# Layer 2's attention scores: half-size batches, each split, turned and copied several chunks ahead of its first use

## The reference, cut to what matters

```python
z = jnp.einsum('ni,hif->nhf', h, W)
el = jnp.einsum('nhf,hf->nh', z, a_l)
er = jnp.einsum('nhf,hf->nh', z, a_r)
e = jax.nn.leaky_relu(el[src] + er[dst], NEG_SLOPE)
m = jax.ops.segment_max(e, dst, num_segments=N)
ex = jnp.exp(e - m[dst])
s = jax.ops.segment_sum(ex, dst, num_segments=N)
alpha = ex / s[dst]
out = jax.ops.segment_sum(alpha[:, :, None] * z[src], dst, num_segments=N)
```

## Time and profile before

| what | us |
| --- | --- |
| median of 3 runs | 3153.91 (3153.67 to 3155.99) |
| the profiled execution | 3143.41 |
| its span, first to last instruction | 3141.5 |
| chunk 0's first reduce on DVE | starts at 1286.10 |
| chunk 351's last fold into `by_node` | starts at 1719.99, two instructions, 0.36 |
| first gather of the next stage on POOL | starts at 1722.49 |

### The profile page before, as it was taken

How to read it: one execution, slowest core, us unless ns; L and a number is a source line. 1 busy time by engine, 2 the same in 40 slices (tenths; PEclk the granted TensorE clock), 3 DMA queues, 4 the chain that set the end, 5 groups by cost and what they waited for, 6 DMA issues and landing times. The chain is left out here.

```text
span 3141.5 us, 50069 instructions
## 1 busy us (share of the span) xinstructions
PE 2774.9 (88%) x13690; PEld 2153.1 (69%) x13690; DVE 2489.0 (79%) x5349; ACT 1571.3 (50%) x3053; POOL 1639.9 (52%) x1473
## 2 busy tenths in 40 slices
PE   4999969999996997998988999999999595599997
PEld 3788734444445776776766788888888484488886
DVE  8656769999997676577777999999999785577775
ACT  3555623333334525333333677777777451266664
POOL 1788746666663572777773444444444230044443
PEclk9999989999998998999999999999999797699999
DMA  5433489999992032111111778778877551499997
GB/s 184 113 93 107 143 303 347 348 350 353 349 335 59 1 134 55 36 23 23 22 23 34 260 261 259 260 260 261 260 263 255 175 201 58 183 297 297 289 293 194
DMA packets 193609, 609.60 MB, mean 194 GB/s; under 512 B 41979, under 2 KB 51570, under 8 KB 189758
## 3 DMA queue, kind: packets, MB, share of 16 engines
q0 software_dynamic: 135040, 429.23, 43.3%
q1 hardware_dynamic: 58430, 178.63, 16.2%
HBM read 522.69 MB, written 84.86 MB: 193 GB/s over the span
## 5 line engine op out<-in xcount | busy, mean ns | idle before, releaser
L649 POOL DMA_INDIRECT g_rows<-z_rows,edge_src x704 | 696.6, 990 | 608.5 <-PE g_totals L1473 314.7
L1090 POOL DMA_INDIRECT shared<-el_rows,edge_src x352 | 336.7, 957 | 179.6 <-issue 107.0
L690 ACT ACTIVATE g_scaled_hi<-g_rows,edge_weight_sorted 128x1024 fp32r<-128x1024 f32 x176 | 202.7, 1151 | 355.3 <-DMA g_rows<-z_rows,edge_src 345.3
L704 PE MATMUL g_sums<-g_rows,g_share 128*128 128x512 f32 x704 | 332.2, 594 | 22.9 <-DMA g_rows<-z_rows,edge_src 22.9
L1466 PE MATMUL g_sums<-g_rows,g_share 128*128 128x256 f32 x1408 | 348.9, 391 | 0.0
L321 POOL DMA_INDIRECT edge_list<-payload,row_i x196 | 260.6, 1330 | 124.6 <-issue 115.9
L1418 ACT ACTIVATE g_scaled_hi<-g_rows,g_factor 128x256 fp32r<-128x256 f32 x704 | 299.9, 496 | 4.3 <-DMA g_rows<-z_rows,edge_src 2.1
L1542 DVE SCALAR_TENSOR_TENSOR g_scaled_lo<-g_rows,g_factor,g_scaled_hi 128x256 fp32r<-128x256 f32 x704 | 293.4, 479 | 1.7 <-ACT g_scaled_hi L1418 1.6
L1466 PEld LDWEIGHTS g_sums<-g_rows,g_share 128*128 128x128 f32 x1408 | 255.4, 191 | 27.8
L1321 DVE TENSOR_REDUCE t_largest<-t_masked 128x4 f32<-128x512 f32 x352 | 231.5, 685 | 51.9 <-PE t_masked L1172 44.6
L725 DVE SCALAR_TENSOR_TENSOR g_scaled_lo<-g_rows,edge_weight_sorted,g_scaled_hi 128x1024 fp32r<-128x1024 f32 x176 | 225.5, 1281 | 47.3 <-ACT g_scaled_hi L690 44.1
(11 more groups left out here) (396 smaller groups left out, 7494.1 us busy)
## 6 DMA issues: line engine op xcount, KB each, us to landing
e_raw<-in_L_ffn_rw_dram SPq DMA_DIRECT2D x56, 1024.0 KB, 6.8
g_rows<-z_rows,edge_src POOLq DMA_INDIRECT x704, 5.6
z_rows<-z_zout SPq DMA_DIRECT2D x20, 512.0 KB, 3.1
x_rows<-x_all SPq DMA_DIRECT2D x20, 512.0 KB, 2.6
z_rows<-t_zout SPq DMA_DIRECT2D x20, 512.0 KB, 2.7
s_x<-x_rows SPq DMA_DIRECT2D x20, 512.0 KB, 7.1
xn_rows<-s_rows SPq DMA_DIRECT2D x10, 1024.0 KB, 4.1
z_x<-in_x_dram SPq DMA_DIRECT2D x19, 512.0 KB, 4.1
```

The costliest lines, as they stand in the source:

```text
L649: pool.indirect_dma_start(out=r.rows[:, slot, :], out_offset=None, in_=table, in_offset=bass.IndirectOffsetOnAxis(ap=g.src[:, i * GT + q:i ...
L704: nc.tensor.matmul(sums[:, k, h, :], share[:, k, :], r.rows[:, k * GT, h * HALF:(h + 1) * HALF], start=True, stop=False)
L1090: q.indirect_dma_start(out=g.edge_el[:, n, :], out_offset=None, in_=g.el, in_offset=bass.IndirectOffsetOnAxis(ap=g.src[:, n:n + 1], axis=0 ...
```

## The change

Layer 2's batches become smaller and are prepared earlier:

- `BATCH` is 16; `BATCHES` lists the sizes: 21 batches of 16 and two of 8, so 23 in place of 11. `BATCH_AT` is the first chunk of each, `BATCH_OF` the batch of each chunk.
- A batch's three steps no longer stand at its first chunk `at`: the split on DVE stands ahead of take `at`-7, the turn on PE ahead of mask `at`-5, the copy on ACT ahead of chunk `at`-4's `set_apart`.
- `Z_FIRST` is 80 in place of 160, and the remaining 880 products are spread up to chunk 343 (`spread` = 344).

POOL's instructions are the same; only the semaphores that the landings count on differ.

```diff
-BATCH = 32
-NB = NE // BATCH
+BATCH = 16
+BATCHES = (BATCH,) * (NE // BATCH - 1) + (BATCH // 2, BATCH // 2)
+NB = len(BATCHES)
+BATCH_AT = tuple(sum(BATCHES[:b]) for b in range(NB))
+BATCH_OF = tuple(b for b in range(NB) for _ in range(BATCHES[b]))
+SPLIT_BEFORE = {max(0, at - 7): b for b, at in enumerate(BATCH_AT)}
+TURN_BEFORE = {max(0, at - 5): b for b, at in enumerate(BATCH_AT)}
+COPY_BEFORE = {max(0, at - 4): b for b, at in enumerate(BATCH_AT)}
...
-Z_FIRST = 160
+Z_FIRST = 80
...
-    spread = NE - BATCH // 2
+    spread = NE - BATCHES[-1]
...
-                ).then_inc(el_in[n // BATCH], 16)
+                ).then_inc(el_in[BATCH_OF[n]], 16)
...
-                b = n // BATCH
-                if n % BATCH == 0:
+                b = BATCH_OF[n]
+                if n == BATCH_AT[b]:
                     pe.wait_ge(rows_ready, b + 1)
...
-                    if n % BATCH == 0:
-                        turn_rows(n // BATCH)
+                    if n in TURN_BEFORE:
+                        turn_rows(TURN_BEFORE[n])
                     mask_chunk(n)
...
-                at_least(act, masked_ready, BATCH * (b - 1))
+                at_least(act, masked_ready, BATCH_AT[b - 1] if b else 0)
...
-                    if n % BATCH == 0:
-                        rows(n // BATCH)
+                    if n in COPY_BEFORE:
+                        rows(COPY_BEFORE[n])
...
-                dve.wait_ge(el_in[b], 16 * BATCH)
+                size = BATCHES[b]
+                dve.wait_ge(el_in[b], 16 * size)
...
-                    if n % BATCH == 0:
-                        parts(n // BATCH)
+                    if n in SPLIT_BEFORE:
+                        parts(SPLIT_BEFORE[n])
                     take(n)
```

More of the change, by code:

```diff
@@ L1171, in mask_chunk @@
                          start=True, stop=False)
-                t.matmul(masked[:, n % 3, :], pick[:, n % BATCH:n % BATCH + 1].to_broadcast([P, P]), el_rows[:, b % 2, :], start=False, stop=True).then_inc(masked_ready, 1)
+                t.matmul(masked[:, n % 3, :], pick[:, n - BATCH_AT[b]:n - BATCH_AT[b] + 1].to_broadcast([P, P]), el_rows[:, b % 2, :], start=False, stop=True).then_inc(masked_ready, 1)
             turn_tile(0, NT)
@@ L1310, in parts @@
             def parts(b):
-                dve.wait_ge(el_in[b], 16 * BATCH)
+                size = BATCHES[b]
+                dve.wait_ge(el_in[b], 16 * size)
                 at_least(dve, rows_turned, b - 1)
-                whole = g.edge_el[:, b * BATCH:(b + 1) * BATCH, :].rearrange("p n h -> p h n")
-                st.link(v.tensor_copy(el_parts[:, b % 2, :, 0, :], whole))
-                v.tensor_tensor(el_parts[:, b % 2, :, 1, :], whole, el_parts[:, b % 2, :, 0, :].bitcast(F32),
+                whole = g.edge_el[:, BATCH_AT[b]:BATCH_AT[b] + size, :].rearrange("p n h -> p h n")
+                st.link(v.tensor_copy(el_parts[:, b % 2, :, 0, 0:size], whole))
+                v.tensor_tensor(el_parts[:, b % 2, :, 1, 0:size], whole, el_parts[:, b % 2, :, 0, 0:size].bitcast(F32),
                                 ALU.subtract).then_inc(parts_ready, 1)
```

## The result

The changed kernel took 3136.14 us (median of 6 runs, 3128.98 to 3143.10) against 3153.79 for the kernel before (6 runs, 3145.50 to 3156.34). The ratio is 0.9948 with a 95% interval of 0.9928 to 0.9968: 17.7 us less, with an interval of about 10 to 23. The forecast was 13.4 less, 3140.5.

The account below looks back on a forecast made before the run. Gathers were taken to bind up to take 313: chunk 335 lands at 1660.9, then 45.4 us of work and 0.7 of lag end the stage at 1707.0 against 1720.35. That is 13.4 us less, 3140.5; range 3129 to 3148.

Parts of the forecast that it names:

- Which engine binds: In the chunk stage, gathers at 20.1 us per 16 chunks bind up to take 313; DVE and PE work sets the rest.
- The rate: DVE and PE work per batch of 16 chunks in the new order: 19.4 us, against 20.1 for the gathers.
- The coupling: DVE and PE coupled by three banks only: waits inside batches, 0.6 us per 16 chunks.
- PE's extra share: PE's share in a batch of 16 chunks grows by 3 matmuls, 0.7 us.
- the slack: Up to take 313, DVE's time spent waiting for gathers: 11 us over 20 boundaries, 0.7 us each.
- The last stretch: From chunk 335's landing: batch 20's split, then chunks 313 to 351, 45.4 us, with 0.7 of lag added.
- lag: Lateness left over from PE's half clock, added to the end of the stage: 0.7 us.
- The start: First reduce on DVE at 1269.7 in place of 1286.10, 16.4 us earlier, with 80 fewer products ahead of chunk 0.
- The first (gathers bind to the last): Rival: take 337 waits for the very last gather; stage ends at 1695.2, 25 us less, 3128.8; under 3136, chance 0.17.
- The second (gain given back at 20.5 per 16): Rival: engines run late throughout at 20.5 us per 16 chunks; 2 us less, 3152; within 6 us, chance 0.09.
- The third (half clock behind each boundary): Rival: each of 21 gather waits costs 3.1 us through the clock; 40 us more, 3194; over 6 us slower, chance 0.05.
- My argument against the rival: If DVE is late for the gathers, it does not wait; PE's stand shrinks to the split's 0.5 us, clock stays.

Follow-up runs that it names:

- the lead alone: Changed kernel with 11 batches of 32 and 160 leading products, spread up to chunk 335: stage 485.1 us, whole 3149.30, ratio 0.9982 to the kernel before.
- 160 leading products: Changed kernel with `Z_FIRST = 160` in place of 80: stage 466.5 us against 471.2, whole 3139.10 in one run.
- The removal of the waits: Changed kernel with splits reading a constant tile, DVE waiting for all gathers only behind the last chunk: stage 451.8 us against 471.2, whole 3116.20.
- kernel without a lead: Changed kernel with split, turn and copy at a batch's first chunk again: stage 537.2 us, whole 3202.31, ratio 1.0136 to the kernel before.
- the two kernels made for it: Changed kernel with 104 leading products, spread to chunk 319, or 160, spread to 311: 3561.98 and 3569.44 us on slow chips, 0.9902 and 0.9927 of the kernel before.

## Why the prediction was right

**Which engine binds.** Predicted: gathers to take 313, then work. Measured: 15 waits for landings, the last one ahead of take 313, none at takes 329 and 337 (1680.08 and 1689.62). In time: take 313's split at 1660.16 - 1233.12 = 427.0 us behind the first gather, predicted 1660.9 - 1235.8 = 425.1. It is 1.9 late. 1.1 of it is POOL's beat: the last gather was issued 443.9 behind the first in place of 442.8. The rest is the landing: chunk 335's gather started at 1656.87 and the split 3.3 us later, where I took the median of 2.4; with the lead alone and with 160 leading products the same distance was 3.2. The removal of the waits (451.8) and the late start that cost nothing (466.5) show the step, not only its numbers.

**The rate.** I took 19.4 us per 16 chunks. Measured 19.1 beside gathers, 18.8 without them, and 18.4 with 37 products per 16 chunks in place of 41 (the run's own expectation says 38). The coupling and PE's extra share, 0.6 and 0.7 of it, were a little too high. I had sized the slack accordingly too small, 11 us over 20 boundaries or 0.7 each; it was 24.6 in 15 waits, 1.6 each. This moves no term of the sum, since the landing of chunk 335's gather sets take 313 either way.

**The last stretch.** Predicted 45.4 and 0.7 of lag, measured 44.2. It began at half clock (0.88 over the 14 us from 1658 to 1672), so the lag was real, and the sum without it 1 to 2 us too long, as the rate is.

**The sum.** 425.1 + 46.1 = 471.2 predicted, 427.0 + 44.2 = 471.2 measured. That they agree to a tenth is luck: +1.9 and -1.9 cancel. The whole moved by 17.7 where 13.4 was carried over, within the interval of about 10 to 23; the stage can't tell what the 4 us are, and the rest of the program varies by more than that between executions.

**The start.** Predicted 16.4 earlier; 50.3 - 34.7 = 15.6 behind the first gather. It entered nowhere in the sum, and rightly: the run with 160 leading products shows it to be worth nothing here.

**Terms.** A split took 0.5 (0.22 and 0.26, overlapping slightly in the next), the turn 0.6 to 0.75. Both as taken.

**The rivals.** The first (gathers bind to the last) didn't come: behind take 313, 43.7 us of work remain even without gather waits. The second (gain given back at 20.5 per 16) needed the clock to cost as much per boundary as before; it cost less, 9 us at 1.2 GHz in place of 28. The third (half clock behind each boundary) did not happen in the changed kernel, 0.99. In the kernel without a lead, 0.94, the clock fell behind 16 of 20 boundaries, though at about 1.2 us of loss each (60 x 0.455 over 22) and not the 3.1 of the rival; that its 3202 us lie near the rival's 3194 is luck, since the stops came back too. The Trainium skill, "TensorE: Matmul & The Clock Gate", HAM oscillation, describes a loop in which each burst of matmuls waits for a transfer and starts again at half rate. The trace agrees in part: in the kernel without a lead most bursts do restart so, but what they wait for is DVE and ACT; in the changed kernel, with as many batches, transfers are waited for and the clock falls behind 2 of 22 boundaries. My argument against the rival, that where DVE is late PE's stand shrinks and the clock stays, is borne out by the kernel without gather waits (3.9 us of stands, clock 0.99). It needs the lead: without it PE stood 40.7 us for splits though no gather was waited for.

## What to carry to other kernels

Here a transfer stream ran a few per cent slower than the engines (20.1 against 19.1 us per 16 chunks). Taking out the stops between the engines then only moved the wait to the stream, until the batches shrank too. In both kernels with the lead the last wait that binds stands ahead of take 313, with 39 chunks behind it. With batches of 32 it was for the last gather of all, 445.6 us behind the first; with batches of 16 it was for the gather 16 earlier, 427.0 behind. So look for the last wait that binds, ask which transfer it is for, and count the work after it. A step that is prepared several items ahead brings its wait for data forward with it; small batches keep that wait short. Whether filler work, here the products of z, should stand ahead of that wait and not behind it is an expectation from the same reckoning; the two kernels made for it did not settle it.

## What the runs showed of the hardware

- With two stops of PE per boundary, about 1.9 us for the split (40.7 us in 22) and 0.67 for the copy, the granted clock was 0.94 over 503 us. With one stop, of up to 2.6 us, at 13 boundaries, it was 0.99 over 436 us. With one stop of 3.1 us on average at 10 boundaries it was 0.96 over 437 us. For the kernel without a lead I had priced only the stops.
- A gather's data were used 3.2 to 3.3 us behind its start at the waits that were looked at, where the median from start to landing in the profile is 2.4.
- On some chips the same program ran 14% longer, 3598 us. There, in the traces of the changed kernel's variants, the unrolled stage issued one matmul per 2.80 us at 1.2 GHz beside POOL's stream of indirect DMAs, and ran at its usual rate, 18.8 us per 16 chunks, within 55 us of the last gather. The cause was not found.
